# A decoder's stage ahead of attention, in a new order: one variant of raw keys, heads on halves of the array

## The chip, the cores and the metric

The kernel runs on one core of a Trainium2 chip. The metric is device time in microseconds of one launch. The kernel before was timed in three runs: 939.58, 941.70 and 941.96 us, median 941.7.

## The reference

Two decoder layers over 8 sequences of 128 tokens, 256 features wide, all in float32 unless noted. What matters here is the attention of the first layer, self-attention (A) and cross-attention (X), and both in their form with low-rank keys and values:

```python
# A: x is the layer's input, normed (mean and variance)
kv = x @ wkv_a                       # 256 -> 64 latent + 64 rotary
kv_c, k_pe = kv[..., :64], kv[..., 64:]
kv_dec = rms_norm(kv_c, kv_norm_w) @ wkv_b      # per head: 64 key, 128 value
q_pe, k_pe = apply_rope(q_pe), apply_rope(k_pe)
attn = softmax(causal(q @ k * scale));  out = (attn @ v) @ out_proj_w   # 16 heads
# X: ctx is the other input
kv_c = kv @ W_kvc;  k_rope = rope(kv_c @ W_kr)
q_nope = (q @ W_dq) @ W_uq;  k_nope = kv_c @ W_uk;  v = kv_c @ W_uv
good = (k_ids <= seg) & (k_ids >= seg - 8)
out = (softmax(where(good, scores, -1e30)) @ v) @ W_o
```

The remaining parts (a mixture of 32 experts, then a state-space block, a recurrent block and a quantised feed-forward block) aren't touched by the change.

## The kernel before

The kernel is one program with one memory arena of 128 partitions. It consists of blocks; inside a block each engine runs its own instruction list, tied to the others by semaphores, and all engines meet at a block's end. The first block is the stage ahead of attention; the second is attention, written out as a pipeline of slots. The first block prepares, for X and for A:

- `key`, in two versions: version 0 has the latent keys on partitions 0 to 63 and the rotated keys on 64 to 127, version 1 has them the other way round (even and odd heads of attention use one each). TensorE computes three variants of raw keys per half of 512 tokens (`pe_key_raw`, L266): latent with rotary part, the two exchanged, and the rotary part with its pairs swapped, twice. Each variant is two matmuls over 128 input features; one float32 matmul leaves two records in the trace. VectorE (`dve_keys`) multiplies the first two by the cosine table (L287), the third by the sine table (L290), and adds (L293, L294). The cosine table holds ones for the latent part.
- for A, the latent keys are then scaled by the root of their mean square: ScalarE squares (L315), TensorE sums over partitions with a matrix of ones (L272), VectorE adds the epsilon (L299), ScalarE takes the root (L317), VectorE the reciprocal (L301) and two products (L303, L305), half by half.
- `kvn`, the latent keys turned to tokens on partitions (`pe_key_tokens` L277, `act_key_tokens` L321).
- `wq`, the absorbed queries: per head the query weights times the key weights, for X (L486, evacuated at L451) and for A (L501, L462). For A it is 64 records: 16 heads times two chunks of 128 features, with operands on partitions 0 to 63.
- `wvo`, the value weights times the output weights, 32 heads in 16 rounds of two (L520). The value weights are stored twice side by side, so that each product of 128 columns gives both halves; ScalarE keeps partitions 0 to 63 of one (L468) and VectorE 64 to 127 of the other (L440), in two PSUM banks.
- the norm of x (class `Norm`): statistics and aggregation on VectorE (L174, L179), root on GpSimd (L206, L208), subtraction and scaling on VectorE (L191), 16 transposes on TensorE (L226), evacuation to `hT` on ScalarE (L240).
- the segment mask on VectorE (L423 to L436).

The order on each engine is the order of the code. VectorE: copies of the key weights of X (L411, four), keys of X, norm, keys of A, mask, value evacuation. TensorE: raw keys of X, absorbed queries of X, tokens of X, norm transposes, raw keys of A half 0, then rounds of absorbed queries of A with the sums of squares and raw keys half 1 between, tokens of A, value products. All loads are issued by SyncE from one list (L329) at the block's start, 27 of them, 13300 KB in total. Attention's slots use the matmuls L615, L625, L634, L643 and L653, and the shuffle L721; L643 has weights of 64 columns that go by turns to the column halves of the array.

Of the kernel before, what the change touches and what calls it, by code (L numbers as in the profile page):

```python
# [6 lines left out]
i32 = mybir.dt.int32  # L7
u32 = mybir.dt.uint32
ALU = mybir.AluOpType
# [58 lines left out]
def decoder(nc, a, out):  # L68
    ctx = ExitStack()
    with ctx:  # L70
# [58 lines left out]
        for name, base, kc, cw in (("A", A0, P, DC), ("X", X0, QC, 1)):  # L129
# [4 lines left out]
            L["wkv"] = view(o, 768, "p (e c m) -> p e c m", e=3, c=DC); o += 768  # L134
# [10 lines left out]
        rawA = W0  # L145
        wqnT = view(rawA, 4096, "p (h f) -> p h f", h=H)
        kbT = view(rawA + 4096, 1024, "p (h r) -> p h r", h=H)
        wvT = {"A": view(rawA + 5120, 2048, "p (h r) -> p h r", h=H)}
        wo = {"A": view(rawA + 7168, 4096, "p (h f) -> p h f", h=H)}
        rawX = rawA + 11264  # L150
        wuqT = view(rawX, 1536, "p (h q) -> p h q", h=H)
        wukT = view(rawX + 1536, 1024, "p (h r) -> p h r", h=H)
        wvT["X"] = view(rawX + 2560, 2048, "p (h r) -> p h r", h=H)
        wkvcT = view(rawX + 4608, 256)
        wkr2 = view(rawX + 4864, 128)
# [91 lines left out]
        class Keys:  # L247


            def __init__(self, tag):  # L250
                self.raw = sem(tag + "_key_raw")
                self.scaled = sem(tag + "_key_scaled")
                self.rotated = sem(tag + "_key_rotated")
                self.sq = sem(tag + "_key_sq")
                self.ssq = sem(tag + "_key_ssq")
                self.inv = sem(tag + "_key_inv")
                self.tok_done = sem(tag + "_kvn_done")
                self.tok = sem(tag + "_kvn")

        def pe_key_raw(eng, L, K, src, half):  # L260

            if half:
                eng.wait_ge(K.scaled, 3)
            for e in range(3):
                for c in range(DC):
                    t = eng.matmul(ps[:, 5 + e, :], L["wkv"][:, e, c, :], src[:, c, half * 512:half * 512 + 512],  # L266
                                   start=c == 0, stop=c == DC - 1)
            t.then_inc(K.raw, 1)

        def pe_key_ssq(eng, K, half):  # L270
            eng.wait_ge(K.sq, half + 1)
            eng.matmul(ps[:, 4, :], ones[0:R, :], keytmp[0:R, 1, :], start=True, stop=True).then_inc(K.ssq, 1)  # L272

        def pe_key_tokens(eng, L, K):
            eng.wait_ge(K.rotated, 2)
            for b in range(NB):
                t = eng.transpose(ps[:, 4, b * R:(b + 1) * R], L["key"][0:R, 0, b * P:(b + 1) * P], ident[0:R, 0:R])  # L277
            t.then_inc(K.tok_done, 1)

        def dve_keys(eng, ch, L, K, rms):  # L280
            for half in range(2):
                ts = slice(half * 512, half * 512 + 512)
                t4 = "p (b t) -> p b t"
                eng.wait_ge(K.raw, half + 1)
                for e in range(2):
                    tab = L["cos"][:, e, :].unsqueeze(1).to_broadcast([P, 4, P])
                    eng.tensor_tensor(L["key"][:, e, ts].rearrange(t4, b=4), ps[:, 5 + e, :].rearrange(t4, b=4),  # L287
                                      tab, ALU.mult).then_inc(K.scaled, 1)
                tab = L["sin"].unsqueeze(1).to_broadcast([P, 4, P])
                eng.tensor_tensor(keytmp[:, 0, :].rearrange(t4, b=4), ps[:, 7, :].rearrange(t4, b=4),  # L290
                                  tab, ALU.mult).then_inc(K.scaled, 1)
                eng.wait_ge(K.scaled, 3 * half + 3)
# [1973 lines left out]
```

## Time and profile before

| | us |
|---|---|
| median of three runs | 941.7 |
| the profiled execution | 941.22 |
| its span | 939.5 |
| stage ahead of attention, end of last evacuation | 82.55 |
| first matmul of attention (L615) | 82.88 |
| mean granted clock of TensorE over the span | 0.894 |

| engine, 0 to 82.8 us | main work |
|---|---|
| TensorE | raw keys (L266) 28.1 us, value products (L520) 15.8, absorbed queries of A (L501) 10.3 |
| VectorE | reciprocals (L301) 6.7, value evacuation (L440) 6.8, products with cosine (L287) 5.2 |
| ScalarE | value evacuation (L468) 6.0, two table loads 2.6 |

Times are counted from the start of the span. A row of a timeline reads: start, duration, engine, line, operation, output and input, number of records merged, and in brackets the idle time ahead of it with what ended it. TensorE's records overlap in its pipeline, so that the time from one start to the next is less than one record's duration. A granted clock of 1.00 is 2.4 GHz and 0.50 is 1.2 GHz.

### The profile page before, as it was taken

To read this page: it belongs to the slowest core of one execution; us is meant where nothing else is said; L and a number is where in the kernel's file an instruction comes from. 1 tells how busy PE (TensorE), PEld (TensorE's weight loads), DVE (VectorE), ACT (ScalarE), POOL (GpSimd) and SP (SyncE) were. 2 spreads that over 40 slices of the span, in tenths; PEclk is the share of its full clock that TensorE was granted. 3 is DMA by queue.
4 is the path that set the end of the run, shared out by engine and by line. 5 is a ranking of instruction groups with operands and counts; after the bars stand their busy time and mean duration, and the time that the engine had idled before them with its cause. 6 is when DMAs were issued, how large, how long until landed. Compare 5 with 4: busy or idle time off the path is not lost. (4 is left out here: it accounts for less than half of the span.)

```text
span 939.5 us, 14653 instructions
## 1 busy us (share of the span) xinstructions
PE 761.6 (81%) x4330; PEld 545.1 (58%) x4333; DVE 728.4 (78%) x1554; ACT 537.9 (57%) x1381; POOL 521.4 (55%) x541
## 2 busy tenths in 40 slices
PE   6798999999999988459999717977999999950265
PEld 2467888888888876247777503335555555540133
DVE  1484878789889887567777676678999999779887
ACT  0223555556556555236666442798899788218185
POOL 1001768777777776135555177825888788523211
PEclk9779999999999999759999957988999999985576
DMA  8804400000000040045455523021232232010000
GB/s 285 295 0 175 185 1 2 1 7 2 7 7 1 8 192 7 12 171 179 145 148 142 108 81 98 2 91 46 90 112 90 90 108 94 1 45 0 1 17 29
DMA packets 30077, 72.20 MB, mean 77 GB/s; under 512 B 5648, under 2 KB 19728, under 8 KB 27504
## 3 DMA queue, kind: packets, MB, share of 16 engines
q1 hardware_dynamic: 25392, 58.67, 17.4%
q0 software_dynamic: 4608, 12.59, 5.6%
q8 instruction: 37, 0.61, 0.3%
q14 instruction: 40, 0.33, 0.1%
HBM read 60.70 MB, written 10.55 MB: 76 GB/s over the span
## 5 line engine op out<-in xcount | busy, mean ns | idle before, releaser
L1815 POOL TENSOR_TENSOR arena<-arena 128x1024 f32<-128x1024 f32 x63 | 148.5, 2386 | 43.1 <-DVE arena L1737 43.1
L1737 DVE TENSOR_TENSOR_SCAN arena<-arena,ps 128x1024 f32<-128x1024 f32 x64 | 143.7, 2277 | 11.4 <-PE ps L1462 7.3
L1483 PE MATMUL ps<-arena 128*128 128x512 f32 x256 | 120.1, 592 | 0.0
L812 ACT ACTIVATE arena<-arena 128x128 f32<-128x128 f32 x256 | 98.8, 390 | 12.4 <-DVE arena L736 12.2
L615 PE MATMUL ps<-arena 128*128 128x128 f32 (+1 forms) x768 | 100.5, 281 | 0.8 <-PEq L346 0.8
L1044 POOL DMA_INDIRECT arena<-tokens,arena x64 | 62.4, 975 | 69.5 <-PE ps L1072 51.5
L615 PEld LDWEIGHTS ps<-arena 128*128 128x128 f32 (+1 forms) x768 | 91.4, 193 | 13.7 <-issue 12.1
L820 ACT ACTIVATE arena<-ps 128x512 f32<-128x512 f32 x64 | 38.2, 597 | 87.7 <-PE ps L634 87.7
L1610 ACT ACTIVATE arena<-arena 128x1016 f32<-128x1016 f32 x64 | 72.3, 1135 | 19.1 <-DVE arena L1737 19.0
L1625 ACT ACTIVATE arena<-arena 128x256 f32<-128x256 f32 x192 | 81.3, 494 | 0.1
L863 POOL TENSOR_TENSOR arena<-arena 128x512 f32<-128x512 f32 x64 | 66.6, 1041 | 21.5 <-DVE arena L742 21.5
L625 PEld LDWEIGHTS ps<-arena 128*128 128x128 f32 x512 | 68.4, 196 | 8.9 <-POOL arena L859 5.5
L625 PE MATMUL ps<-arena 128*128 128x128 f32 x512 | 69.8, 280 | 4.5 <-POOL arena L859 4.5
L1084 PE MATMUL ps<-arena 128*128 128x128 f32 x512 | 73.2, 287 | 0.2 <-issue 0.2
L853 POOL TENSOR_TENSOR arena<-arena 128x256 f32<-128x256 f32 x64 | 47.6, 744 | 45.7 <-DVE arena L722 45.6
L653 PE MATMUL ps<-arena 128*128 128x256 f32 x256 | 66.8, 384 | 5.3 <-DVE arena L747 5.3
L1462 PEld LDWEIGHTS ps<-arena 128*128 128x128 f32 x384 | 45.1, 144 | 39.4 <-DVE arena L1737 21.0
L1084 PEld LDWEIGHTS ps<-arena 128*128 128x128 f32 x512 | 64.0, 196 | 3.7 <-issue 1.2
L1483 PEld LDWEIGHTS ps<-arena 128*128 128x128 f32 x256 | 45.2, 190 | 35.6 <-issue 33.3
L1462 PE MATMUL ps<-arena 128*128 128x128 f32 x384 | 52.1, 281 | 11.1 <-ACT arena L1625 7.0
L719 DVE TENSOR_TENSOR arena<-ps,arena 128x512 f32<-128x512 f32 x64 | 43.5, 679 | 18.5 <-PE ps L615 17.8
L731 DVE TENSOR_TENSOR arena<-ps,arena 128x512 f32<-128x512 f32 x64 | 43.8, 684 | 17.7 <-PE ps L625 17.7
(319 smaller groups left out, 1670.6 us busy)
## 6 DMA issues: line engine op xcount, KB each, us to landing
arena<-c_rows SPq DMA_DIRECT2D x32, 512.0 KB, 3.5
arena<-in_E_gu SPq DMA_DIRECT2D x8, 1024.0 KB, 11.9
expert_out<-arena SPq DMA_DIRECT2D x64, 128.0 KB
arena<-in_E_dn SPq DMA_DIRECT2D x1, 4096.0 KB, 12.2
arena<-in_ctxT SPq DMA_DIRECT2D x2, 1024.0 KB, 4.9
arena<-in_X_o SPq DMA_DIRECT2D x1, 2048.0 KB, 19.4
arena<-in_A_o SPq DMA_DIRECT2D x1, 2048.0 KB, 26.7
arena<-in_F_w SPq DMA_DIRECT2D x2, 1024.0 KB
```

Source lines behind the costliest of these rows:

```text
L615: t = eng.matmul(ps[:, i % 2, j * P:(j + 1) * P], L["wq"][0:L["kc"], c, GH * g + j, :], src[0:L["kc"], c, b * P:(b + 1) * P], start=c == 0 ...
L625: t = eng.matmul(ps[:, 2 + i % 2, j * P:(j + 1) * P], q[:, i % NG, j, :], layer[name]["key"][:, j % 2, b * P:(b + 1) * P], start=True, sto ...
L653: t = eng.matmul(ps[:, BANK_O[name], 0:D], uT[:, i % 2, j, :], layer[name]["wvo"][:, GH // 2 * g + j, :], start=g == 0 and j == 0, stop=g ...
L812: t = eng.activation(pr[:, i % 3, j, :], sm[:, d, j, :], ACT.Exp, bias=negm[:, d, j:j + 1], scale=SCALE[slots[i][0]], accum_out=rsum[:, i ...
L863: eng.tensor_tensor(pr[:, i % 3], pr[:, i % 3], rinv[:, i % 3].unsqueeze(2).to_broadcast([P, GH, P]), ALU.mult).then_inc(pr_ready, 1)
L1084: t = eng.matmul(ps[:, 2 + d, k * I:(k + 1) * I], wcur[:, d, c, k * I:(k + 1) * I], xinT[:, d, c, :], start=c == 0, stop=c == DC - 1)
L1462: t = eng.transpose(psD[d][:, b // 4, at:at + P], sT[:, j % 2, b, k * P:(k + 1) * P], ident)
L1483: t = eng.matmul(ps[:, 2 * k + r, :], ident, half(hC[s % 4], r), start=False, stop=n == ST - 1)
L1610: eng.activation(dA[s % 4].rearrange(t8, b=NB)[:, :, 1:P], dts[:, c].rearrange(t8, b=NB)[:, :, 1:P], ACT.Exp, scale=negA[:, ST * c + n:ST ...
L1625: eng.activation(sT[:, j % 2, b, :], dtuT[:, b, 2 * cp:2 * cp + 2, :].rearrange("p c m -> p (c m)"), ACT.Copy, scale=B_tok[:, b, n:n + 1]) ...
L1737: eng.tensor_tensor_scan(hst[s % 4], dA[s % 4], psD[s % 2].rearrange("p k m -> p (k m)"), 0.0, ALU.mult, ALU.add).then_inc(h_ready, 1)
L1815: eng.tensor_tensor(hC[s % 4], hst[s % 4], Csb[i % 4], ALU.mult).then_inc(hC_ready, 1)
```

## The change

All of it is in the first block, its buffers and the host's preparation of weights.

- Raw keys: one variant in place of three, two matmuls per half. X's halves go to PSUM banks 5 and 6, A's to 7 and 4. VectorE's `stream_shuffle` swaps the pairs, then three operations on 64 partitions give the rotated keys in version 0. ScalarE copies place the latent and the rotated keys in version 1.
- The root takes scale and epsilon in the activation (with a new constant, `rms_eps`), and works, as the reciprocal, on 64 partitions. One product per half.
- Absorbed queries of A: the operands of even heads lie on partitions 0 to 63, of odd heads on 64 to 127; the heads alternate, and write to banks 2 and 3, one chunk of features at a time. The first chunk is done ahead of the norm's transposes.
- Value products: value weights stored once, 64 columns; even heads go to output partitions 0 to 63 and odd to 64 to 127; eight rounds of four heads, in four banks, A's first; ScalarE evacuates the even rounds, VectorE the odd.
- The mask comes first on VectorE. The norm's statistics come ahead of X's first rotation, its subtraction between X's two.
- The loads: segment ids fourth from the start, A's key weights, tables and absorbed operands ahead of X's absorbed operands, A's value weights ahead of X's. 11940 KB in place of 13300.

```diff
-            L["wkv"] = view(o, 768, "p (e c m) -> p e c m", e=3, c=DC); o += 768
+            L["wkv"] = view(o, 256, "p (c m) -> p c m", c=DC); o += 256
...
         def pe_key_raw(eng, L, K, src, half):
-            if half:
-                eng.wait_ge(K.scaled, 3)
-            for e in range(3):
-                for c in range(DC):
-                    t = eng.matmul(ps[:, 5 + e, :], L["wkv"][:, e, c, :], src[:, c, half * 512:half * 512 + 512],
-                                   start=c == 0, stop=c == DC - 1)
+            for c in range(DC):
+                t = eng.matmul(ps[:, K.banks[half], :], L["wkv"][:, c, :], src[:, c, half_of[half]],
+                               start=c == 0, stop=c == DC - 1)
             t.then_inc(K.raw, 1)
...
+        def dve_key_rope(eng, L, K, half):
+            ts, t4 = half_of[half], "p (b t) -> p b t"
+            raw, own, swapped = ps[R:P, K.banks[half], :], L["key"][R:P, 0, ts], keytmp[R:P, half, :]
+            eng.wait_ge(K.raw, half + 1)
+            eng.stream_shuffle(swapped, raw, swap_pairs).then_inc(K.parts, 1)
+            eng.tensor_tensor(own.rearrange(t4, b=4), raw.rearrange(t4, b=4),
+                              L["cos"][R:P, 0, :].unsqueeze(1).to_broadcast([R, 4, P]), ALU.mult).then_inc(K.parts, 1)
+            eng.wait_ge(K.parts, 2 * half + 1)
+            eng.tensor_tensor(swapped.rearrange(t4, b=4), swapped.rearrange(t4, b=4),
+                              L["sin"][R:P].unsqueeze(1).to_broadcast([R, 4, P]), ALU.mult).then_inc(K.turned, 1)
+            eng.wait_ge(K.parts, 2 * half + 2)
+            eng.wait_ge(K.turned, half + 1)
+            eng.tensor_tensor(own, own, swapped, ALU.add).then_inc(K.rotated, 1)
+
+        def dve_key_rms(eng, L, K, half):
+            eng.wait_ge(K.root, half + 1)
+            eng.reciprocal(keytmp[0:R, half, :], keytmp[0:R, half, :]).then_inc(K.inv, 1)
+            eng.wait_ge(K.inv, half + 1)
+            eng.scalar_tensor_tensor(L["key"][0:R, 0, half_of[half]], ps[0:R, K.banks[half], :], kv_norm[0:R, :],
+                                     keytmp[0:R, half, :], ALU.mult, ALU.mult).then_inc(K.latent, 1)
...
+        def act_key_place(eng, L, K, half, latent=False):
+            ts = half_of[half]
+            eng.wait_ge(K.rotated, half + 1)
+            eng.activation(L["key"][0:R, 1, ts], L["key"][R:P, 0, ts], ACT.Copy).then_inc(K.placed, 1)
+            if latent:
+                eng.wait_ge(K.latent, half + 1)
+                eng.activation(L["key"][R:P, 1, ts], L["key"][0:R, 0, ts], ACT.Copy).then_inc(K.placed, 1)
...
             @block.vector
             def _(eng):
...
+                loaded(eng, "x")
+                normA.dve_begin(eng, 0)
+                loaded(eng, "ropeX")
+                dve_key_rope(eng, LX, keysX, 0)
+                eng.wait_ge(keysX.raw, 2)
+                normA.dve_end(eng, 0)
+                dve_key_rope(eng, LX, keysX, 1)
+                loaded(eng, "kvA", "ropeA")
+                for half in range(2):
+                    dve_key_rope(eng, LA, keysA, half)
+                for half in range(2):
+                    dve_key_rms(eng, LA, keysA, half)
+                for n in range(1, H // 2, 2):
+                    vo_evacuate(eng, n)
...
             @block.scalar
             def _(eng):
+                for half in range(2):
+                    act_key_latent(eng, LX, keysX, half)
...
+                absorbed(0)
+                normA.act(eng)
+                for half in range(2):
+                    act_key_place(eng, LX, keysX, half)
+                eng.wait_ge(s_const, 13)
+                for half in range(2):
+                    act_key_square(eng, keysA, half)
+                absorbed(1)
+                for half in range(2):
+                    act_key_root(eng, keysA, half)
+                act_key_tokens(eng, LX, keysX, 5)
...
+                act_key_tokens(eng, LA, keysA, 3)
+                for half in range(2):
+                    act_key_place(eng, LA, keysA, half, latent=True)
+                for n in range(0, H // 2, 2):
+                    vo_evacuate(eng, n)
...
             @block.tensor
             def _(eng):
...
+                def absorb(c):
+                    eng.wait_ge(absA_ready, 2 * c)
+                    for q in range(H // 2):
+                        for e in range(2):
+                            rows = slice(e * R, (e + 1) * R)
+                            t = eng.matmul(ps[:, 2 + e, q * R:(q + 1) * R], wqnT[rows, q, c * P:(c + 1) * P], kbT[rows, q, :],
+                                           start=True, stop=True)
+                    t.then_inc(absA_done, 1)
+
+                loaded(eng, "absA")
+                absorb(0)
                 normA.pe(eng)
                 eng.wait_ge(normA.hT_ready, 4)
                 loaded(eng, "kvA")
...
+                for half in range(2):
+                    pe_key_raw(eng, LA, keysA, hT, half)
+                absorb(1)
+                for half in range(2):
+                    pe_key_ssq(eng, keysA, half)
+                pe_key_tokens(eng, LX, keysX, 5, 4)
+                loaded(eng, "absX")
...
+                pe_key_tokens(eng, LA, keysA, 3, 2)
+                for n in range(H // 2):
+                    name, m = ("A", n) if n < 4 else ("X", n - 4)
...
+                    for pair in range(2):
+                        for e in range(2):
+                            head = 4 * m + 2 * pair + e
+                            t = eng.matmul(ps[e * R:(e + 1) * R, VO_BANK[n % 4], pair * D:(pair + 1) * D],
+                                           wvT[name][:, head, :], wo[name][:, head, :], start=True, stop=True)
                     t.then_inc(vo_done, 1)
```

## Rows read from the trace of the kernel before

**Rows 1.** The page, part 2: granted clock in 40 slices, tenths.
```profile
PEclk9779999999999999759999957988999999985576
```
**Rows 2.** Busy time by stretch: stretch and length, engines, granted clock, DMA share, GB/s.
```profile
...
18.00:20.00 2.00, 1.69 (x4) 0.87 (x5) 1.63 (x3) 0.00 (x0) 0.00 (x0) 1.00 0.82 164
...
32.00:34.00 2.00, 0.71 (x4) 0.68 (x5) 1.18 (x4) 0.00 (x0) 0.78 (x1) 0.50 0.98 418
...
42.00:44.00 2.00, 2.00 (x6) 0.86 (x5) 0.00 (x0) 0.00 (x0) 0.00 (x0) 1.00 0.09 13
...
60.00:62.00 2.00, 2.00 (x11) 1.91 (x10) 2.00 (x1) 0.73 (x3) 0.00 (x0) 0.50 0.00 0
```
**Rows 3.** Timeline of TensorE's matmuls, 0 to 115 us.
```profile
7.84 8.42 PE L266 MATMUL ps<-arena 128*128 128x512 f32 x12 [3.08 <-DMA arena<-in_X_kvc]
18.32 5.42 PE L266 MATMUL ps<-arena 128*128 128x512 f32 x12 [2.06 <-DVE arena L290]
...
37.81 7.11 PE L266 MATMUL ps<-arena 128*128 128x512 f32 x12 [0.69 <-ACT arena L240]
44.85 2.00 PE L501 MATMUL ps<-arena 64*128 64x64 f32 x16
46.69 1.07 PE L272 MATMUL ps<-arena 64*128 64x512 f32 x2
...
64.54 1.11 PE L277 MATMUL ps<-arena 64*128 64x64 f32 x8 [0.73 <-DVE arena L305]
65.58 3.45 PE L520 MATMUL ps<-arena 128*128 128x256 f32 x8
69.76 12.32 PE L520 MATMUL ps<-arena 128*128 128x256 f32 x56 [0.73 <-DVE arena L440]
82.88 3.81 PE L615 MATMUL ps<-arena 128*128 128x128 f32 x32 [0.79 <-PEq L346]
```
**Rows 4.** Timeline of VectorE, 0 to 110 us.
```profile
17.58 0.68 DVE L290 TENSOR_TENSOR arena<-ps,arena 128x512 f32<-128x512 f32 x1
...
27.29 2.71 DVE L174 BATCH_NORM_STATS2 arena<-arena 128x6 f32<-128x256 f32 x8
...
32.82 2.67 DVE L191 TENSOR_SCALAR arena<-arena 128x256 f32<-128x256 f32 x8 [2.15 <-POOL arena L208]
...
59.56 3.35 DVE L301 RECIPROCAL arena<-arena 128x512 f32<-128x512 f32 x1 [0.69 <-ACT arena L317]
...
63.73 0.75 DVE L305 SCALAR_TENSOR_TENSOR arena<-arena 64x512 f32<-64x512 f32 x1
...
64.78 1.66 DVE L426 TENSOR_SCALAR arena<-arena 128x128 f32<-128x128 f32 x8
...
82.12 0.43 DVE L440 COPY arena<-ps 64x256 f32<-64x256 f32 x1 [0.43 <-PE ps L520]
...
85.65 0.45 DVE L721 STREAM_SHUFFLE arena<-ps 64x256 f32<-64x256 f32 x1
```
**Rows 5.** Timeline of ScalarE, 0 to 110 us.
```profile
46.39 1.28 ACT L317 ACT_TABLE_LOAD   x1
49.02 0.63 ACT L317 ACTIVATE arena<-arena 128x512 f32<-128x512 f32 x1 [1.34 <-DVE arena L299]
```
**Rows 6.** SyncE's DMA issues in order of time, and their time to landing.
```profile
5.10 0.43 SPq L329 DMA_DIRECT2D arena<-in_x  x1
...
6.05 0.43 SPq L329 DMA_DIRECT2D arena<-in_X_ukT  x1
...
arena<-in_x SPq DMA_DIRECT2D x1, 1024.0 KB, 5.7
...
arena<-in_X_ukT SPq DMA_DIRECT2D x1, 512.0 KB, 7.9
```
**Rows 7.** By line, attention's L643 and L653: duration min/median/max, first and last start.
```profile
L643 PE MATMUL ps<-arena x4: 379/404/431, 102.1 to 102.3; 128*64 128x256 f32 x4
...
L653 PE MATMUL ps<-arena x4: 379/379/382, 105.0 to 105.6; 128*128 128x256 f32 x4
```

More of the change, by code:

```diff
@@ new lines, in dve_key_rms, with act_key_latent @@
+        def dve_key_rms(eng, L, K, half):
[4 more added lines that the diff above has]
+                                     keytmp[0:R, half, :], ALU.mult, ALU.mult).then_inc(K.latent, 1)
+        def act_key_latent(eng, L, K, half):
+            eng.wait_ge(K.raw, half + 1)
+            raw = ps[0:R, K.banks[half], :]
+            eng.activation(L["key"][0:R, 0, half_of[half]], raw, ACT.Copy).then_inc(K.latent, 1)
+            eng.activation(L["key"][R:P, 1, half_of[half]], raw, ACT.Copy).then_inc(K.latent, 1)
@@ new lines, in act_key_square, with act_key_root @@
+        def act_key_square(eng, K, half):
+            eng.wait_ge(K.raw, half + 1)
+            eng.activation(keytmp[0:R, half, :], ps[0:R, K.banks[half], :], ACT.Square).then_inc(K.sq, 1)
+        def act_key_root(eng, K, half):
+            eng.wait_ge(K.ssq, half + 1)
+            eng.activation(keytmp[0:R, half, :], ps[0:R, half, :], ACT.Sqrt, bias=rms_eps[0:R, :],
+                           scale=1.0 / R).then_inc(K.root, 1)
+        def act_key_place(eng, L, K, half, latent=False):
[5 more added lines that the diff above has]
+                eng.activation(L["key"][R:P, 1, ts], L["key"][0:R, 0, ts], ACT.Copy).then_inc(K.placed, 1)
@@ L499, in _ @@
+                pe_key_tokens(eng, LX, keysX, 5, 4)
+                loaded(eng, "absX")
+                for g in range(2):
+                    if g:
+                        eng.wait_ge(absA_ready, 4)
                     for j in range(8):
                         hd = 8 * g + j
-                        t = eng.matmul(ps[:, k % 2, j * R:(j + 1) * R], wqnT[0:R, hd, c * P:(c + 1) * P],
-                                       kbT[0:R, hd, :], start=True, stop=True)
-                    t.then_inc(absA_done, 1)
@@ L504, in _ @@
[L504 to L521 removed]
+                        t = eng.matmul(ps[0:QC, ABSX_BANK[g], j * R:(j + 1) * R], wuqT[:, hd, :], wukT[:, hd, :],
+                                       start=True, stop=True)
```

231 lines of the change are left out of this document (80 added, 151 removed).

## The prediction

> **What bounds the kernel now.** The change touches only the stage ahead of attention, so I looked at where that stage ends and what happens behind it. The page first: TensorE's granted clock is full in most slices, with a dip to 7 in the second [rows 1]. The busy shares by stretch say what that dip is, and that the loads are over by about 42 us, while the stage goes on for another 40 [rows 2]. So its second half is a matter of engines, not of DMA. The timeline of TensorE then gives the order: raw keys, absorbed queries, norm, raw keys of A, absorbed queries of A, tokens, and 16 rounds of value-times-output products, until attention's first matmul at 82.88 us [rows 3]. VectorE's timeline shows what interrupts it: key work that ends only at 64.5 us (63.73 + 0.75), with a reciprocal of 3.35 in each half of A, and the segment mask right behind it at 64.78 [rows 4]. In the last 17 us TensorE is busy without a break and both evacuating engines wait for it [rows 3, 4]. Attention and all behind it start when the last evacuation ends, so a microsecond off the stage should be a microsecond off the kernel; nothing behind it depends on absolute time except the clock.
>
> **Basis.** The profiled execution took 941.22 us, 1.72 more than its span of 939.5. The median of the runs is 941.7, 0.5 more again. I build the new end of the stage and subtract.
>
> **The new order, step by step.**
> *Raw keys of X.* One variant in place of three: 4 records per half, not 12. The start stays near 7.84 us, since 1172 KB are issued up to ctxT and before it was 1248 KB up to the last kvX load. The first 12 records took 8.42 us, the next 12 took 5.42 (0.45 each) [rows 3]. Eight records that begin slowly end at about 15. The single copy of the key weights in place of four saves 0.6 us that the wait for ctxT hides anyway.
> *VectorE up to h.* The mask now comes first: 1.7 us plus three long operations, some 4.5 us in all [rows 4], between about 5.5 and 10.5. It is hidden by the load of x, issued at 5.10 and landed 5.7 later, at 10.8 [rows 6]; with fewer bytes ahead of it x might be 0.5 sooner. Without that cover the mask would cost up to 4.5. Then statistics and aggregation 3.4 (27.29 to the start of the idle time before 32.82) [rows 4] to 14.2. Then the first half of X's rotation: a shuffle of 64x512 from PSUM, for which the nearest row is 0.45 at 64x256, so 0.45 to 0.9, I take 0.8; and three operations at 0.69: 2.9 in all, to 17.1. The GpSimd root (2.15) is hidden behind it [rows 4]. Subtraction 2.7 [rows 4]: h is complete at 19.8, against 35.5 before.
> *absA.* It moves ahead of absX, on all 128 partitions. Up to it 3988 KB are queued. Before, 3744 KB had landed with ukT at 6.05 + 7.9 = 13.95 us [rows 6]; the other 244 KB at some 400 GB/s (the stretch from 32 us moved 418 [rows 2]) make 14.6. TensorE reaches absorb(0) at about 15, so this wait ends at once. Queued behind the wait, should it last, are normA's transposes, due only at 17.5: 2.5 us of slack.
> *Absorbed queries of A.* 64 records as before; 16 took 2.00 us, 0.125 each, on rows 0 to 63 alone [rows 3]. Now even and odd heads alternate on the row halves. No row shows row halves; the nearest is the value product of attention on column halves, whose four records all start within 0.2 us, where four on the full array start over 0.6 [rows 7]. So 32 records cost between 2.0 and 4.0 us at full clock; I take 2.5, nearer the row of halves. absorb(0) ends by 17.5, its two evacuations by 18.8, off the path.
> *Transposes and hT.* From the end of the subtraction to the next raw keys it was 37.81 - 35.49 = 2.3 us [rows 3, 4]; unchanged: 22.1.
> *Raw keys of A.* 8 records in a row in place of 24 broken up. 3.6 at 0.45 each; before, 12 records here took 7.11 against 5.42, 1.7 more, because TensorE entered them at a granted 0.50 (1.2 GHz) [rows 2, 3]. I add the same 1.7: 27.4. Bounds 3.6 (all at 2.4 GHz) and 7.5 (all at 1.2 GHz).
> *absorb(1)* 2.5: 29.9. *ScalarE:* two evacuations of 128x512 at about 0.6, the table load 1.28, the first root 0.63 [rows 5]: 33.1. The first sum of squares (1.07 [rows 3]) is hidden behind the evacuations; this wait is new, for absorb(1) now stands ahead of the sums.
> *VectorE:* twice reciprocal and product, 3.35 + 0.75 [rows 4], 8.2 with no gap since the second root is long done: 41.4. The additive step from PSUM (0.68) is gone, folded into the root; one of two products per half is now a ScalarE copy. TensorE does X's tokens and the absorbed queries of X meanwhile, and then waits some 5 us, so it enters the last part at half clock.
> *Tokens of A* 1.1 [rows 3]: 42.6. ScalarE then has one copy and four placements ahead of its first value evacuation, 5 x 0.6 = 3 us; with four banks for the rounds this delays only round 4, due at about 48, and costs nothing. The placements cross partitions, which no row shows; bounds 0.3 and 1.2 each, hidden either way.
> *Values times output.* Before: 56 records in 12.32 us, 0.22 each at full clock, and the first 8 in 3.45, 0.43 each [rows 3]. 64 remain, now on column halves: exactly the shape of L643 (128x64 weights, 256 columns) [rows 7]. A pair of heads, four records, costs 0.43 when perfectly side by side and 0.87 when not. I take 0.47: 16 pairs make 7.5 us, and 2 more for the part at half clock. End 52.1. The evacuation is 128x512 per four heads, about 0.7, on alternating engines, half the time of a round, so it keeps up; the last adds 0.8: 52.9. The hand-over to attention was 0.33 (82.12 + 0.43 to 82.88) [rows 3, 4]: 53.2.
> *Queue of SP.* Everything that it moves is ahead of its own uses: voA and voX have 10388 KB issued up to them and land near 31 us at that rate, 10 before their use; the q loads are later but due only at the end.
>
> **Sum.** 82.88 - 53.2 = 29.7 us less. 941.2 - 29.7 = 911.5, and on the footing of the median 912.
>
> **Two rules weighed.** The matmuls of L643 overlap on the two column halves [rows 7]. The Trainium skill (TensorE: Matmul & The Clock Gate, Part 3) says that a weight load overlaps a running matmul only where the row groups differ, which would leave the loads of column halves exposed; with 0.05 us per record as an estimate from half the page's load price, the last part would be 3.2 longer, 915. The four matmuls of L643 start within 0.2 us although each has a load of its own [rows 7], so the loads can't be exposed by much, and I don't follow it. The same skill (TensorEngine Tiling (Array Packing), Performance Considerations) warns that evacuation becomes the bound after tiling. Here a round of four heads gives each engine two rounds' time for one evacuation of 0.7, so by the rows it does not.
>
> **Rivals.**
> (a) *The halves don't run side by side* in long alternating streams: the change then doesn't do that part of what it says. absorb(1) costs 1.5 more, the last part 16 x 0.87 = 13.9 for 7.5: +7.9, 920. For: no row shows such a stream. Against: L643 in every slot of attention. 9%.
> (b) *Half clock from the raw keys of A to the end:* +2.2, +1.5 and +5.5, 921. For: the clock stood at 0.50 both after idle time (32 us) and while 64-wide matmuls kept TensorE busy (60 us) [rows 2], and the new order has much of both. Against: 56 records of L520 ran at full clock once they were dense. 9%.
> (c) *absA late.* Before, the stretch around 18 us moved only 164 GB/s [rows 2]. If such a dip fell on absA, 6 us late, TensorE would stand 3.5 past its slack: 916. For: the dip exists. Against: it came with the loads to 64 partitions alone, which are gone. 7%.
> (d) *Full clock throughout:* 1.7 + 2 less, 908. 10%.
> (e) *Slower than before.* Attention follows a sparser stage. If it then ran at half clock, each microsecond of it that TensorE bounds costs half a microsecond; the change is lost from 60 us on, and with 80 us at half clock the time is 912 + 40 = 952. For: the stage's own dip shows how a sparse stretch loses the clock. Against: in attention it then stayed at 9 and more for a dozen slices [rows 1]. 2%.
> The forecast itself has 60%; 3% are for what I have not seen.
>
> **How the numbers follow.** Low end: (d) with 2.0 for absorb and 0.43 per pair, x sooner, and 2 us of clock luck behind the stage: 904. High end: (a) or (b), 921. What one measurement of this kernel can tell from no change is about 0.3%, 3 us. All cases but (e) and some of the unseen are faster by more: 0.96; 0.02 and 0.02 for the others.
>
> **What would show it.** h complete near 20; raw keys of A begin near 22; root at 33; the second product near 41; first value round near 43; rounds of 0.95 once the clock is back; attention's first matmul near 53; everything behind it the same to 2 us. The prediction is wrong if the last part is bound by evacuation, if the wait for absA is seen, or if attention's own length changes.

## The result, and the profile after

The changed kernel takes 910.42 us (median of four runs, 906.78 to 911.05) against 941.44 for the kernel before: a ratio of 0.9666, 95% interval 0.9637 to 0.9695. The forecast was 912, in a range of 904 to 921. The profiled execution took 911.05 us with a span of 909.3, which is 30.2 less than before. Medians are of fast runs, and one run of the kernel with the mask last (mask_late), which took 2848.71 us, is left out of its median.

TensorE's timeline of the changed kernel, as [rows 3]. Its columns: start, duration, line, shape, records, and in brackets the idle time ahead.

```profile
8.39 5.14 PE L273 MATMUL ps<-arena 128*128 128x512 f32 x8 [3.74 <-DMA arena<-in_ctxT]
16.95 2.61 PE L517 MATMUL ps<-arena 64*128 64x64 f32 x32 [3.42 <-DMA arena<-in_A_kbT]
19.50 3.84 PE L230 MATMUL ps<-arena 128*128 128x128 f32 x16
24.02 5.86 PE L273 MATMUL ps<-arena 128*128 128x512 f32 x8 [0.69 <-ACT arena L244]
29.81 2.00 PE L517 MATMUL ps<-arena 64*128 64x64 f32 x32
...
43.19 1.11 PE L285 MATMUL ps<-arena 64*128 64x64 f32 x8 [6.01 <-DVE arena L306]
44.23 9.41 PE L556 MATMUL ps<-arena 128*64 128x256 f32 x64
54.98 3.73 PE L649 MATMUL ps<-arena 128*128 128x128 f32 x32 [1.35 <-PEq L371]
```

Attention's first matmul moved from 82.88 to 54.98 us, 27.9 earlier. The raw keys of A (L273 at 24.02, before L266 at 37.81) start 13.8 earlier. From there to the first value product it is 20.2 us for 27.8, and from that to the last evacuation 10.2 for 17.0. Two waits stand out: 3.42 for A's absorbed operands and 6.01 for the scaled keys. VectorE's timeline, as [rows 4]:

```profile
12.12 2.71 DVE L178 BATCH_NORM_STATS2 arena<-arena 128x6 f32<-128x256 f32 x8 [2.65 <-DMA arena<-in_x]
...
15.54 0.73 DVE L292 STREAM_SHUFFLE arena<-ps 64x512 f32<-64x512 f32 x1
...
18.43 2.68 DVE L195 TENSOR_SCALAR arena<-arena 128x256 f32<-128x256 f32 x8
...
34.97 3.35 DVE L304 RECIPROCAL arena<-arena 64x512 f32<-64x512 f32 x1 [1.66 <-ACT arena L321]
38.35 0.74 DVE L306 SCALAR_TENSOR_TENSOR arena<-ps,arena 64x512 f32<-64x512 f32 x1
39.02 3.33 DVE L304 RECIPROCAL arena<-arena 64x512 f32<-64x512 f32 x1
42.39 0.74 DVE L306 SCALAR_TENSOR_TENSOR arena<-ps,arena 64x512 f32<-64x512 f32 x1
```

The clock by stretches of 2 us, as [rows 2] (the column before the last two is the granted clock):

```profile
18.00:20.00 2.00, 2.00 (x21) 1.88 (x20) 1.97 (x6) 0.39 (x1) 0.00 (x0) 0.54 1.02 417
...
24.00:26.00 2.00, 1.98 (x3) 0.95 (x4) 0.00 (x1) 1.14 (x2) 0.00 (x0) 0.50 0.93 387
...
40.00:42.00 2.00, 0.00 (x0) 0.00 (x0) 2.00 (x1) 0.00 (x0) 0.00 (x0) 0.50 0.00 0
...
46.00:48.00 2.00, 2.00 (x12) 1.17 (x10) 0.04 (x1) 1.93 (x4) 0.00 (x0) 0.50 0.00 0
...
50.00:52.00 2.00, 2.00 (x22) 1.30 (x20) 0.73 (x2) 0.60 (x1) 0.00 (x0) 1.00 0.00 0
```

In the stage the clock falls to 1.2 GHz twice. The first time is at 18 to 20 us, behind the wait of 3.42, and the norm's transposes and over half of the raw keys of A run at 1.2 GHz. The second time is in the long wait: while VectorE makes its two reciprocals TensorE does nothing, its clock falls, and the first half of the value products runs at 12 records per 2 us where the second half has 22.

The other 2.3 us of the 30.2 were gained behind the stage, in code that the change doesn't touch. SyncE's stores of tokens in attention show most of it, first before, then after (start, time from the first of four to the last's end):

```profile
329.25 0.33 SPq L329 DMA_DIRECT2D arena<-in_E_dn  x1
...
344.95 42.31 SPq L601 DMA_DIRECT2D tokens<-arena  x4
```

```profile
300.88 0.33 SPq L342 DMA_DIRECT2D arena<-in_E_dn  x1
...
316.59 40.71 SPq L635 DMA_DIRECT2D tokens<-arena  x4
```

Up to 300 us the kernels are 28.4 apart; then the last four stores take 40.71 us for 42.31. That 1.6 us is taken up below; what the 0.5 between 27.9 and 28.4 came from isn't known.

### The profile page after: what moved, and what is told of

The parts are those of the page before. It is cut to its first block and busy times, and to the rows that moved or that the text cites. A ratio compares the mean times of both kernels' runs of the same rounds, so it can differ in the third digit from the quotient of the medians.

```text
span 909.3 us, 14551 instructions
## 1 busy us (share of the span) xinstructions
PE 728.5 (80%) x4298; PEld 523.7 (58%) x4301; DVE 716.4 (79%) x1535; ACT 540.0 (59%) x1375; POOL 521.6 (57%) x542
## 5 line engine op out<-in xcount | busy, mean ns | idle before, releaser
L1849 POOL TENSOR_TENSOR arena<-arena 128x1024 f32<-128x1024 f32 x63 | 148.5, 2383 | 43.1 <-DVE arena L1771 43.1
L1771 DVE TENSOR_TENSOR_SCAN arena<-arena,ps 128x1024 f32<-128x1024 f32 x64 | 143.7, 2276 | 11.4 <-PE ps L1496 7.3
L1118 PE MATMUL ps<-arena 128*128 128x128 f32 x512 | 72.1, 284 | 0.2 <-issue 0.2
L659 PE MATMUL ps<-arena 128*128 128x128 f32 x512 | 68.4, 277 | 4.1 <-POOL arena L893 4.1
L1118 PEld LDWEIGHTS ps<-arena 128*128 128x128 f32 x512 | 63.0, 194 | 3.5 <-issue 0.9
L1496 PE MATMUL ps<-arena 128*128 128x128 f32 x384 | 52.1, 281 | 11.1 <-ACT arena L1659 7.0
## 6 DMA issues: line engine op xcount, KB each, us to landing
arena<-in_X_o SPq DMA_DIRECT2D x1, 2048.0 KB, 21.6
```

Source lines behind the costliest of these rows:

```text
L659: t = eng.matmul(ps[:, 2 + i % 2, j * P:(j + 1) * P], q[:, i % NG, j, :], layer[name]["key"][:, j % 2, b * P:(b + 1) * P], start=True, sto ...
L1118: t = eng.matmul(ps[:, 2 + d, k * I:(k + 1) * I], wcur[:, d, c, k * I:(k + 1) * I], xinT[:, d, c, :], start=c == 0, stop=c == DC - 1)
L1496: t = eng.transpose(psD[d][:, b // 4, at:at + P], sT[:, j % 2, b, k * P:(k + 1) * P], ident)
L1771: eng.tensor_tensor_scan(hst[s % 4], dA[s % 4], psD[s % 2].rearrange("p k m -> p (k m)"), 0.0, ALU.mult, ALU.add).then_inc(h_ready, 1)
L1849: eng.tensor_tensor(hC[s % 4], hst[s % 4], Csb[i % 4], ALU.mult).then_inc(hC_ready, 1)
```

## The experiments

The question is the same in each: which operation sets when attention starts, and does the kernel follow. All kernels are the changed one with the edit shown. A stage's length depends on where the clock happened to dip in the profiled execution, so the operations are compared one by one where that matters. A profiled execution is one of a kernel's runs, and its stage need not be that of the median.

**Value products, the two heads' order in a round.**

```diff
-                    for pair in range(2):
-                        for e in range(2):
+                    for e in range(2):
+                        for pair in range(2):
```

> Of the changed kernel only the order inside a round of value products differs: both pairs of the even heads, then both of the odd ones, so that the column halves alternate once per round and not per pair of heads. Theory (overlap of neighbours on the two halves pays in this stage): the 64 records of the value products, 9.41 us in the changed kernel, grow, since of the eight records of a round only those at the change of half can overlap; about 1.7 us a round at full clock less one overlap of 0.2 gives 1.3 to 1.5, 10.5 to 13 us in all, and attention's first matmul moves from 54.98 to 57 to 59. Rival (the order of the halves is nothing; rounds are bound by the weight loads or by evacuation): 9.4 us and 55.0 unchanged.

Measured: 910.94 us, and in TensorE's timeline (so in all fences of this section, unless the text says VectorE) the same 64 records in the same time:

```profile
44.15 9.39 PE L556 MATMUL ps<-arena 128*64 128x256 f32 x64
54.70 3.73 PE L649 MATMUL ps<-arena 128*128 128x128 f32 x32 [1.16 <-PEq L371]
```

The theory that neighbours must alternate fell. Either the halves overlap over a distance of four records, or width alone halves the price. The next run decides.

**Value products on one half only.**

```diff
-                            t = eng.matmul(ps[e * R:(e + 1) * R, VO_BANK[n % 4], pair * D:(pair + 1) * D],
+                            t = eng.matmul(ps[0:R, VO_BANK[n % 4], pair * D:(pair + 1) * D],
                                           wvT[name][:, head, :], wo[name][:, head, :], start=True, stop=True)
```

> The changed kernel with all value products going to output partitions 0 to 63, so that only one column half of the array is used and odd heads overwrite even ones (partitions 64 to 127 of wvo are left without their products). In the run with grouped heads the 64 records took 9.39 us as before, which speaks against overlap between the two halves. Theory now (a float32 record with 64 weight columns costs half, wherever it goes; at 256 columns 0.11 us for 0.22): the part keeps 9.4 us with the clock's dip, or 7.1 without. Rival (records on different halves overlap even when grouped, through the queue's reordering): 64 x 0.22 = 13.8 us at full clock, up to 16 with the dip, attention's first matmul at 59 to 61.

Measured (a single run): 917.88 us. The kernel leaves out the products on partitions 64 to 127.

```profile
39.88 1.11 PE L285 MATMUL ps<-arena 64*128 64x64 f32 x8 [6.01 <-DVE arena L306]
40.92 16.16 PE L556 MATMUL ps<-arena 128*64 128x256 f32 x64
```

16.16 us for 9.4, so my second theory fell too and its rival stood: narrow weights are no cheaper (the kernel before paid 0.22 a record at full width, 14.1 us for 64, and the rest is the clock's dip, which both kernels have). The gain comes from the second half working at the same time, and four records of one half followed by four of the other are close enough for it. This is the term "halves side by side" by itself: 6.8 us.

**Absorbed queries, all even heads and then all odd ones.**

```diff
-                    for q in range(H // 2):
-                        for e in range(2):
+                    for e in range(2):
+                        for q in range(H // 2):
```

> Of the changed kernel only the order of the absorbed queries of A differs: per chunk of features all even heads, then all odd ones, so that the row halves alternate once per chunk. Theory (row halves side by side halve the price of a record): the second chunk takes 4.0 us for 2.00 (0.125 a record as in the kernel before), everything behind it is 2.0 later, attention's first matmul at 57.0; the first chunk also takes 4 us, from 16.95 to 21.0, and since the transposes stood directly behind it (idle 0 at 19.50) and the last of h came at 21.1, raw keys of A start up to 0.5 later. Sum 2.0 to 2.7 us. Rival (the price of 0.06 a record came from something else, such as smaller weights in memory): no change.

```profile
17.39 5.23 PE L517 MATMUL ps<-arena 64*128 64x64 f32 x32 [3.63 <-DMA arena<-in_A_kbT]
...
26.71 3.70 PE L273 MATMUL ps<-arena 128*128 128x512 f32 x8 [0.73 <-ACT arena L244]
30.34 3.39 PE L517 MATMUL ps<-arena 64*128 64x64 f32 x32
```

914.35 us, 3.9 above the changed kernel's median. The second chunk took 3.39 for 2.00, less than the 4.0 expected; the first 5.23 for 2.61 and the raw keys of A began 2.7 later. With eight heads of one half in a row (16 records) most of the overlap is gone; why 0.6 of it remained is open. So the row halves are worth 1.4 us per chunk by their order alone. Attention started at 56.16, only 1.2 later, because the raw keys of A met no half clock here (3.70 us for 5.86) and the value products less of it (8.67 for 9.41). The median lost more than the 2 to 2.7 expected; its four runs lie between 911.75 and 919.04, and the rest isn't explained.

**Extra matmuls in the wait for the scaled keys.**

```diff
+                eng.wait_ge(keysA.root, 1)
+                for k in range(6):
+                    eng.matmul(ps[:, 0, :], LA["wkv"][:, 0, :], hT[:, 0, 0:512], start=True, stop=True)
                 pe_key_tokens(eng, LA, keysA, 3, 2)
```

> The changed kernel with six extra matmuls of 128x512, results unused, put where TensorE waits 6.0 us for the scaled keys (37.2 to 43.2 us). Theory (the value products lose 2 us because the clock falls in that wait): the granted clock stays at 1.00 from 30 us on, the 64 records take 7.2 to 7.6 us for 9.41, the tokens of A 0.7 for 1.1, and attention's first matmul comes at 53.0 or a little earlier. The extra work of some 5.4 us ends before the wait does. Rival (the records of the value products are bound by weight loads at any clock): 9.4 and 55.0.

```profile
36.84 5.37 PE L543 MATMUL ps<-arena 128*128 128x512 f32 x12
43.02 0.71 PE L285 MATMUL ps<-arena 64*128 64x64 f32 x8 [0.80 <-DVE arena L306]
43.66 3.67 PE L559 MATMUL ps<-arena 128*64 128x256 f32 x32
47.74 3.67 PE L559 MATMUL ps<-arena 128*64 128x256 f32 x32 [0.41 <-ACT arena L369]
52.47 3.81 PE L652 MATMUL ps<-arena 128*128 128x128 f32 x32 [1.05 <-PEq L371]
```

The tokens take 0.71 for 1.11, the products 7.34 of work for 9.41, and from the tokens' start to attention it is 9.45 us for 11.79: the dip costs some 2.3 us there. A new wait of 0.41 appears, on ScalarE: its five copies ahead of its first value evacuation, which cost nothing at half clock, are now just too long. The kernel's median, 910.13, is only 0.3 lower, which is no difference between runs: a filled wait shortened this stage and not, as far as four runs can show, the kernel. The last table has where executions differ behind the stage.

This execution has a second thing to show. x landed at 11.4 in it, and the subtraction (a line of VectorE's timeline) began 0.8 us before that of the changed kernel; the raw keys of A began 0.3 later all the same:

```profile
17.66 2.68 DVE L195 TENSOR_SCALAR arena<-arena 128x256 f32<-128x256 f32 x8
```

```profile
16.80 3.05 PE L517 MATMUL ps<-arena 64*128 64x64 f32 x32 [1.92 <-DMA arena<-in_A_kbT]
19.78 3.83 PE L230 MATMUL ps<-arena 128*128 128x128 f32 x16
24.30 5.42 PE L273 MATMUL ps<-arena 128*128 128x512 f32 x8 [0.69 <-ACT arena L244]
```

The transposes stand right behind the absorbed queries, at half clock, without waiting for h. The last part uses this.

**Value products moved into the wait.** Rounds in banks 0, 1, 5 and 6, all evacuated by ScalarE, the tokens of A behind them, and VectorE takes the two copies of the scaled latent keys.

```diff
-                pe_key_tokens(eng, LA, keysA, 3, 2)
                 for n in range(H // 2):
...
+                pe_key_tokens(eng, LA, keysA, 3, 2)
                 loaded(eng, "qA", "qX", "gate")
```

> The changed kernel with the value products moved into the wait for the scaled keys of A: rounds in PSUM banks 0, 1, 5 and 6, all evacuated by ScalarE, and the tokens of A last on TensorE; VectorE copies the scaled latent keys to version 1. Theory (the changed kernel's stage is bound by the one chain root, two reciprocals, products, tokens, value products; the last member doesn't depend on the others): TensorE runs on from 37.2 at full clock, eight rounds of 0.87 end near 44.3, tokens by 45.0, attention's first matmul at 46 to 47, the kernel 8 to 9 us shorter than the changed one, near 902. Rival (a microsecond off the stage is given back in attention, whose weights for the experts or whose first slots are due later): first matmul at 46 but a kernel less than 5 us shorter.

```profile
22.53 3.70 PE L273 MATMUL ps<-arena 128*128 128x512 f32 x8 [0.69 <-ACT arena L244]
26.16 2.00 PE L516 MATMUL ps<-arena 64*128 64x64 f32 x32
...
33.45 7.13 PE L555 MATMUL ps<-arena 128*64 128x256 f32 x64
...
42.44 3.84 PE L649 MATMUL ps<-arena 128*128 128x128 f32 x32 [1.22 <-PEq L368]
```

Median 903.17 us, ratio 0.9587 (0.9541 to 0.9633). TensorE has no gap from the raw keys of A to the tokens, which end at 41.22. The granted clock was full in this whole stage, hence 42.4 rather than 46. The fair measure of the move leaves that luck out: from the raw keys of A to attention it is 19.9 us here, and 28.6 to 28.8 in the three unmoved kernels below whose raw keys of A took 3.70 us too (mask_late, x_first, norm_first). The move is worth 8.8 us of the stage, and the other 3.7 of the 12.5 come from where the clock stood before. The span (900.8) is 8.5 shorter and the median 7.3. The 4.0 that the span lacks are read off the trace: 1.1 more gained at attention's start, 1.6 lost over its last stores, 1.4 in the experts' input matmuls, and 2.2 from there to the end.

**Two more variants of raw keys of A**, unused, in banks 0 and 1.

```diff
+            if K is keysA:
+                for bank in range(2):
+                    for c in range(DC):
+                        t = eng.matmul(ps[:, bank, :], L["wkv"][:, c, :], src[:, c, half_of[half]],
+                                       start=c == 0, stop=c == DC - 1)
             t.then_inc(K.raw, 1)
```

> The changed kernel with two extra variants of raw keys of A, results unused, in banks 0 and 1, so that TensorE's work there is as in the kernel before. Theory (A's raw keys stand on the chain, one for one): 24 records for 8, 16 x 0.45 = 7.2 us more at full clock, less up to 1 us since the longer dense stretch lifts the clock earlier in its course: attention's first matmul 6 to 7.5 later, at 61 to 62.5, the kernel near 917. Rival (VectorE's rotation of A hides them, as it has slack): under 3 us.

915.74 us, 5.3 above the changed kernel.

```profile
23.61 1.98 PE L273 MATMUL ps<-arena 128*128 128x512 f32 x4 [0.69 <-ACT arena L244]
25.43 3.60 PE L278 MATMUL ps<-arena 128*128 128x512 f32 x8
...
34.11 2.00 PE L522 MATMUL ps<-arena 64*128 64x64 f32 x32
```

From 23.61 to 34.11 is 10.5 us; the one variant at the same clock takes 3.63 (22.53 to 26.16 above). The 16 extra records cost 6.9, on the chain. Attention started only 4.2 later than in the changed kernel, outside the 6 to 7.5 that I gave, because there the eight records had met the half clock (5.86) and here none did.

**The mask last on VectorE, as before.** Its block of operations stands behind the scaled keys of A.

```diff
                 for half in range(2):
                     dve_key_rms(eng, LA, keysA, half)
+                loaded(eng, "seg")
...
                 for n in range(1, H // 2, 2):
                     vo_evacuate(eng, n)
```

> The changed kernel with the segment mask back behind the scaled keys of A on VectorE, ahead of its value evacuations. The 4.6 us of mask would run from 43.1 to 47.8; VectorE's first evacuation is due at 47.96. Theory (moving the mask to the front gained nothing as such, it has cover in either place): attention's first matmul within 0.3 of 55.0. Rival (each microsecond of VectorE's counts because it holds the chain): 4.6 us later, 59.6, near 915.

```profile
43.06 1.23 DVE L458 TENSOR_TENSOR arena<-arena 128x1024 f32<-128x1024 f32 x1
44.62 0.69 DVE L367 COPY arena<-ps 128x512 f32<-128x512 f32 x1 [0.34 <-PE ps L556]
```

These are lines of VectorE's timeline. It stood idle for 0.34 us between the mask's last operation and its first evacuation, waiting for TensorE, so the mask is hidden in this place too. 911.63 us (median of three runs), 1.2 above the changed kernel, within what runs differ. Attention started at 51.53, outside the 0.3 around 55.0 that I gave, since the raw keys of A took 3.70 us here; from their start to attention it is 28.69 us, against 28.64 in x_first below, where the mask stands first. Putting the mask first gained nothing by itself.

**X's absorbed operands ahead of A's in the load list.**

```diff
+                load(eng, "absX", wuqT, a["X_uqT"])
+                load(eng, "absX", wukT, a["X_ukT"])
                 load(eng, "absA", wqnT, a["A_qnT"])
                 load(eng, "absA", kbT, a["A_kbT"])
-                load(eng, "absX", wuqT, a["X_uqT"])
-                load(eng, "absX", wukT, a["X_ukT"])
```

> The changed kernel with the two loads of X's absorbed operands (1280 KB) issued ahead of A's. Theory (absA lands at 16.95 and TensorE stands for it; the transposes start right behind absorb(0) with no idle time, so it has at most 1.6 us of slack to the last of h at 21.1): 3.3 us later at 400 GB/s, 20.3; absorb(0) to 22.9, transposes and hT, now one dense run, end near 26.5 rather than 24.0: 2 to 2.5 us later, first matmul near 57.3. Rival (slack hides it, as the prediction's 2.5 us had it): under 0.8 us.

```profile
19.34 3.18 PE L517 MATMUL ps<-arena 64*128 64x64 f32 x32 [4.80 <-DMA arena<-in_A_kbT]
22.45 3.84 PE L230 MATMUL ps<-arena 128*128 128x128 f32 x16
26.98 3.70 PE L273 MATMUL ps<-arena 128*128 128x512 f32 x8 [0.69 <-ACT arena L244]
```

A's operands came 2.4 later, at 19.34, and the raw keys of A began 3.0 later, at 26.98: no slack at all. So the load order is worth about 3 us at this place, and the changed kernel as it stands is held at 16.95 by this load. Attention started 1.2 later (56.13), as the raw keys of A took 3.70 us. The median is 917.70 us, 7.3 above the changed kernel; in the profiled execution 4.4 of the 5.9 us that its span is longer lie behind attention, and the cause of that is open.

**x ahead of ctxT; and, in another kernel, the subtraction ahead of X's first rotation.**

```diff
+                load(eng, "x", x, a["x"])
                 load(eng, "ctx", ctxT0, a["ctxT"])
...
-                load(eng, "x", x, a["x"])
```

```diff
-                dve_key_rope(eng, LX, keysX, 0)
                 eng.wait_ge(keysX.raw, 2)
                 normA.dve_end(eng, 0)
-                dve_key_rope(eng, LX, keysX, 1)
+                for half in range(2):
+                    dve_key_rope(eng, LX, keysX, half)
```

> The changed kernel with the load of x issued ahead of that of ctxT (1024 KB each). In the changed kernel x landed at 12.1 us, 1.3 later than the prediction had it, and everything up to the value products was about as much later. Theory (h waits for x through VectorE alone): x lands near 8, under the mask, and statistics run 9.5 to 12.9; but raw keys of X then begin near 11.5 for 8.4, their first half ends near 15, and X's first rotation, ahead of the subtraction, waits for it: subtraction from 18.0, h complete at 20.7 for 21.1, attention's first matmul 0 to 0.7 earlier at equal clock. Rival (x's landing is the whole of it): h complete at 18.5 to 19, 2 us earlier.

> The changed kernel with the subtraction ahead of X's first rotation on VectorE. Theory (the rotation of 2.9 us filled GpSimd's 2.15 of root and stood 0.8 longer in h's way): h complete at 20.3 for 21.1; the transposes, ready since 19.5, end 0.4 to 0.8 earlier, so does all behind. X's two rotations end at 26, still before A's raw keys at 27.9. First matmul 0.4 to 0.8 earlier at equal clock; the kernel within 1 us of 910.4. Rival (X's first rotation was needed early by somebody): later than before.

The subtraction started at 17.69 with x first (VectorE's statistics at 9.25, then a wait for X's raw keys) and at 17.61 with the norm first, for 18.43. Medians 909.50 and 910.32: 0.9 and 0.1 below the changed kernel, no more than runs differ. h was complete at 20.4 and 20.3, as both theories had it, for 21.1. That this helped anything behind it isn't shown. Attention started at 51.20 and 51.99, but by the clock: the raw keys of A took 3.70 us in both. With x first they began as in the kernel with the value products moved, where h was complete at 20.6 and the load of A's operands landed at the same time (16.99 and 16.95):

```profile
22.56 3.70 PE L273 MATMUL ps<-arena 128*128 128x512 f32 x8 [0.69 <-ACT arena L244]
```

**Both of these and the moved value products together.**

> All three edits at once: value products in the wait for A's scaled keys, x ahead of ctxT, subtraction ahead of X's rotations. Theory: the subtraction begins when the raw keys of X are read from ctxT, near 16.5, h complete at 19.2, transposes behind absorb(0) end near 21.5, raw keys of A from 22.3 for 24.0, and from there as in the run with the value products moved (20 us from raw keys of A to attention's first matmul at full clock, 23 with a dip): first matmul at 42 to 45, the kernel at 900 to 903. Rival (the move alone has all of it, as absA's landing at 16.95 and TensorE's own work bind next): 903, same as the move alone.

```profile
19.12 2.00 PE L516 MATMUL ps<-arena 64*128 64x64 f32 x32 [1.74 <-DMA arena<-in_A_kbT]
...
24.69 3.70 PE L273 MATMUL ps<-arena 128*128 128x512 f32 x8 [0.69 <-ACT arena L244]
...
44.48 3.84 PE L649 MATMUL ps<-arena 128*128 128x128 f32 x32 [1.09 <-PEq L368]
```

901.19 us (six runs, 898.31 to 903.90), ratio 0.9589 (0.9563 to 0.9616). It beats both kernels; whether it beats the move alone these runs can't tell (the ratios are alike). h was complete at 20.2, not 19.2, and A's absorbed operands landed at 19.12 in this execution, 2.2 later than in the one with the value products moved, and that is what holds TensorE: the raw keys of A began 5.57 us behind this landing. In x_first it was 5.57 and in vo_in_gap 5.58, although h was complete only 1.0 us behind the landing here and 3.4 and 3.6 there.

**What the clock does behind the stage.** The traces of all these kernels run the same code from attention on. Time from attention's first matmul to the load of E_dn, and time over the last four token stores, against whether the granted clock falls to 0.50 in attention's first 12 us, and again 12 to 18 us into these stores:

| | first matmul to E_dn | last four stores |
|---|---|---|
| falls at the start (before, changed, absorb_grouped, gap_fill, mask_late, x_first, vo_one_half) | 245.9 to 246.4 | |
| full clock at the start (vo_grouped, vo_in_gap, three_variants, absX_first, norm_first, combo) | 244.7 to 244.9 | |
| falls in these stores (before and eight others) | | 42.25 to 42.32 |
| full clock there (changed, vo_one_half, mask_late, x_first) | | 40.70 to 40.71 |

The two dips cost 1.1 to 1.6 and 1.6 us, whatever the kernel. The mixture of experts behind attention took from 116.7 (combo) to 120.9 us (mask_late) between the first and the last of its input matmuls (L1118 of the changed kernel). From the last of them to the end of the span it took between 406.4 (before) and 410.5 us (x_first). I have not tied either to one cause. Each is larger than the two dips, and so a stage 3 us shorter in one profiled execution need not show in the kernel's time.

## Why the prediction was right, point by point

- *Raw keys of X, start and end.* 8.39 and 13.53, against 7.84 and 15. Off the path.
- *h complete at 19.8.* It was 21.1: x landed at 12.1, not at 10.8. I had taken its issue-to-landing time of 5.7 over; in the changed kernel it was 7.3. No more bytes stand ahead of it than before (1364 KB for 1440), but from 4 to 6 us the loads moved 175 GB/s, where in the kernel before they moved 381. VectorE's work behind it came as summed (shuffle 0.73 for the 0.8 taken; 6.3 us from the start of statistics to the subtraction for 6.3).
- *absA at 14.6, the wait over at once.* This is the step that was wrong. The load landed at 16.95, TensorE stood for it for 3.42 us, and the prediction had named this wait as a sign that it would be wrong. The slack of 2.5 us was no slack: the 2.5 us from 15 to 17.5 are absorb(0)'s own time. In the changed kernel the transposes ran from 19.50 right behind absorb(0), 3.84 us at half clock, and no wait for h shows in them. So from 16.95 to the raw keys of A at 24.02 the chain is this load, absorb(0) and the transposes. gap_fill had h 0.8 earlier and no earlier raw keys; absX_first had the load 2.4 later and the raw keys 3.0 later; in vo_in_gap, x_first and combo, at full clock, the raw keys began 5.57 to 5.58 behind the landing, with h complete 1.0 to 3.6 behind it.
- *How much each cost.* The raw keys of A began 1.9 later than the 22.1 of the sum. The late load is enough for all of it, as gap_fill with h at 20.3 shows. The late h would have explained 1.3 by itself, as an estimate: in the kernel before it was 4.99 us from the subtraction's start to the raw keys, and 18.43 + 4.99 is 23.4. In two executions h was the later of the two: the transposes of vo_one_half and three_variants wait 0.65 and 0.62 for VectorE, with h complete at 21.6 and 21.4.
- *absorb(0), absorb(1): 2.5.* 2.61 with the clock falling inside it, and 2.00 at full clock: the lower bound was right. Row halves do overlap; absorb_grouped shows it.
- *Raw keys of A 5.3.* 5.86, from 24.02 for 22.1. The half clock that the sum had was there in this execution and cost 2.2 for the 1.7 taken, but it is a matter of chance: in eight of the other ten traces with eight records they took 3.70.
- *Evacuations, table load, root, reciprocals.* First reciprocal at 34.97 for 33.1, products done at 43.1 for 41.4: about as late as the raw keys of A were, so no new error in this part of the chain.
- *Tokens and value products.* 43.2 to the last evacuation at 54.4 is 11.2 us, the sum had 11.4. The price of 0.47 for a pair of heads was 0.446 at full clock (7.13 / 16), and 2 for the half clock was right: gap_fill took 2.1 of it away. ScalarE's copies cost nothing here, as said; at full clock they would cost 0.4.
- *The hand-over* took 0.6 for 0.33.
- *Attention's first matmul* at 54.98 for 53.2, and *everything behind it the same to 2 us*: it was 2.3 shorter. 1.6 of this was the late dip that this execution did not have. So the two misses, 1.8 in the stage and 2.3 behind it, nearly cancelled in 912 against 910.4, and that is luck. The prediction had also named a change of attention's own length as a sign of being wrong; it came, 0.5 and 1.6 us, the larger by way of the clock.
- *A microsecond off the stage is one off the kernel.* It held here to 2.3 us. It doesn't hold in general for one execution: the moved value products took 12.5 off the stage and 8.5 off the span.
- *What one measurement can tell: 0.3%, 3 us.* Too narrow: runs of one kernel lay up to 7.6 us (0.8%) apart.
- *Rivals.* (a) The halves not side by side: would have given the 16.16 us of vo_one_half; refuted, and with it the 920. Evacuation did not bind the last part, but for the 0.41 in gap_fill. Of the two rules of the Trainium skill that the prediction weighed, the first (TensorE: Matmul & The Clock Gate, Part 3: a weight load overlaps only between row groups), at 915, isn't borne out: 64 records with a load each took 7.13 us on column halves, 0.11 each, half of the 0.22 of full width. The second (TensorEngine Tiling (Array Packing), Performance Considerations) says only that evacuation may become the bottleneck, and here it did not. (b) Half clock throughout and (d) full clock throughout: both partly, as this execution had the dip at the raw keys and at the value products. (c) absA late: it came true by 2.3 us, and there was no slack for it. (e) Attention at half clock: its only dips are the two above.

## What to carry to other kernels

When one stage is a chain over several engines, write down its members with durations from the trace, place the new order on it and read off the waits; a dozen terms summed that way were 1.8 us off in 55, though one of the waits was misjudged. Then look at which member of the chain depends on none of the others: the value products needed only loads and free banks, and moving them into TensorE's one long wait was worth 7 us more (8.8 of the stage), for it filled the wait with their own time and took away the clock's fall in it. Two products that each fill half of the array need not be neighbours in program order: in groups of four records on column halves nothing was lost, in groups of 16 on row halves 1.4 of 2.0 us was. Whether the length of the group or the kind of half makes that difference, no run separates. When you give an engine slack for a late load, count its own work behind that load too.

## What I had not expected of the hardware

- The column halves overlap fully (0.111 us a record of 256 columns against 0.22), and the time is the same with the halves in groups of four records (9.39 us for 9.41); the row halves lose most of it with groups of 16 (3.39 us for 2.00).
- Runs of one kernel lie up to 7.6 us apart (the kernel before in one set of seven: 936.74 to 944.34; absorb_grouped: 911.75 to 919.04). Between profiled executions part of the difference is where the clock dips: at the raw keys of A (5.86 or 3.70 us), at attention's start (1.1 to 1.6) and in its last stores (1.6).
- ScalarE copies a block of 64x512 from PSUM to the other half of the partitions in 0.59 us, the price of one that stays (L313 and L312); from the arena across the halves it takes 0.63.
- The landing time of one load near the head of the list, with 76 KB less ahead, went from 5.7 to 7.3 us (6.8 in vo_in_gap).
